# The first feed-forward bias enters as a 32-row product in PSUM instead of a VectorE step

## What is computed

```python
h = layernorm(x, ln1_g, ln1_b)                    # 256 channels
h = bitlinear(h, w1, b1)                          # 256 -> 1024
h = jax.nn.gelu(h, approximate=False)
h = layernorm(h, ln2_g, ln2_b)                    # 1024 channels
h = bitlinear(h, w2, b2)                          # 1024 -> 256

def bitlinear(x, w, b):     # x rounded to 127 levels per token, w to -1, 0, 1
    return einsum('btd,hd->bth', act_quant_fake(x), weight_quant_fake(w)) + b
```

## Time and profile before

| | before |
|---|---|
| timed runs | 394.05, 397.33, 396.52 |
| median | 396.52 |
| the profiled execution | 393.59, its span 391.8 |
| granted PE clock over the span | 0.995 |
| PE busy | 335.9 (86%) |
| DVE busy | 305.9 (78%) |
| ACT busy | 264.4 (67%) |
| POOL busy | 184.4 (47%) |

### The profile page before, as it was taken

One profiled execution on the slowest core, in us unless ns is written; L12 is line 12 of the kernel. 1 busy time (PEld: TensorE's weight loads), 2 busy tenths in 40 slices (PEclk: granted clock), 3 DMA queues, 4 the chain that ended last, 5 costly groups with the idle time before them and its releaser, 6 DMA issues.

```text
span 391.8 us, 9333 instructions
## 1 busy us (share of the span) xinstructions
PE 335.9 (86%) x3173; PEld 239.8 (61%) x3173; DVE 305.9 (78%) x1026; ACT 264.4 (67%) x567; POOL 184.4 (47%) x207
## 2 busy tenths in 40 slices
PE   7999789999999999967577877867977999999976
PEld 6777566776777677623444554545545666666654
DVE  3998846777898998788999899897346877877884
ACT  2656345466545545757689998988667888888843
POOL 2115301111211375248999899884104555456470
PEclk9999999999999999999899999999999999999999
DMA  7999999979464360000000000000001122212101
GB/s 242 304 271 263 275 239 235 233 151 258 127 127 89 92 99 3 1 2 0 1 3 0 0 2 1 3 0 2 1 2 32 38 43 55 49 37 54 43 14 55
DMA packets 44142, 33.70 MB, mean 86 GB/s; under 512 B 19904, under 2 KB 40256, under 8 KB 43968
## 3 DMA queue, kind: packets, MB, share of 16 engines
q1 hardware_dynamic: 44096, 33.11, 34.5%
HBM read 24.71 MB, written 8.39 MB: 84 GB/s over the span
## 4 chain that ended last, share of the span: by engine, by line
PE 53%; DVE 20%; issue 13%; ACT 8%; POOL 3%; DMA 1%; SPq 0%; DVEq 0%; POOLq 0%; ACTq 0%
PE PS L1340 5%; PE PS L1433 5%; PE PS L1422 4%; PE PS L1670 4%; DVE sm L784 4%; PE PS L1413 4%; PE PS L1412 4%; PE PS L1493 4%; PE PS L1662 4%; PE PS L1452 4%; DVE sm L756 3%; ACT pT L1115 2%; PE PS L1632 2%; PE PS L1655 2%; PE PS L1621 2%
## 5 line engine op out<-in xcount | busy, mean ns | idle before, releaser
L1115 ACT ACTIVATE pT<-PS 128x512 f32<-128x512 f32 x64 | 36.5, 596 | 48.2 <-PE PS L1413 47.9
L645 DVE TENSOR_REDUCE negm<-PS 128x4 bf16<-128x512 f32 x64 | 42.3, 684 | 13.0 <-PE PS L1422 12.8
L445 POOL TENSOR_TENSOR sm<-sm,mhalf 128x1 f32<-128x1 f32 x16 | 11.4, 711 | 80.6 <-DVE sm L677 80.6
L467 POOL TENSOR_TENSOR kst<-kst,rows 128x1024 f32<-128x1024 f32 x16 | 38.0, 2375 | 7.7 <-ACT kst L1159 7.7
L1237 ACT ACTIVATE lnT<-PS,Atok 128x128 f32<-128x128 f32 x128 | 36.4, 369 | 1.9 <-DVE lnb L901 0.8
L1413 PE MATMUL PS<-identb,negm 128*128 128x128 bf16 x256 | 34.9, 220 | 0.0
L1540 PE MATMUL PS<-identf,w2f 128*128 128x128 f32 x128 | 18.3, 288 | 18.2 <-ACT w2f L1182 18.2
L484 POOL TENSOR_TENSOR kst<-kst,rows 128x1024 f32<-128x1024 f32 x14 | 33.2, 2368 | 0.0
L1433 PE MATMUL PS<-pT,vx 128*32 128x128 f32 x512 | 27.0, 285 | 5.2 <-ACT pT L1115 5.2
L1540 PEld LDWEIGHTS PS<-identf,w2f 128*128 128x128 f32 x128 | 14.4, 146 | 22.9 <-ACT w2f L1182 21.5
L512 POOL TENSOR_TENSOR rr<-ms,mhalf 128x8 f32<-128x8 f32 x16 | 26.3, 1648 | 1.9 <-DVE ms L983 1.9
(11 more groups left out here) (228 smaller groups left out, 999.1 us busy)
## 6 DMA issues: line engine op xcount, KB each, us to landing
scr_q<-qpart SPq DMA_DIRECT2D x8, 384.0 KB, 3.4
scr_k<-kpart SPq DMA_DIRECT2D x8, 384.0 KB, 4.5
X<-in_x SPq DMA_DIRECT2D x8, 256.0 KB, 5.1
CTXT<-in_ctxT SPq DMA_DIRECT2D x8, 256.0 KB, 5.2
vx<-in_ctx SPq DMA_DIRECT2D x16, 128.0 KB, 3.1
out<-rest SPq DMA_DIRECT2D x16, 128.0 KB, 1.7
rows<-in_rows SPq DMA_DIRECT2D x1, 1544.0 KB, 10.0
qst<-scr_q SPq DMA_DIRECT2D x8, 192.0 KB, 4.8
```

What stands on the lines that cost most here:

```text
L467: gp.tensor_tensor(n2[q.slot], n2[q.slot], ln2g, ALU.mult).then_inc(b_g2, 1)
L645: v.tensor_reduce(negm[f.slot % 2][:, 4 * hg:4 * hg + 4], PS[:, 2 + hg % 2, :].rearrange("p (h k) -> p h k", h=4), AX_X, ALU.max, negate=T ...
L1115: s.activation(pT[:, hg, :], PS[:, hg % 2, :], ACT.Exp, scale=float(DH0) ** -0.5).then_inc(a_e, 1)
```

## The change

The bias b1 is split into three bfloat16 parts, and so is the reciprocal of each token's scale (unit times mean weight). Six of 32 rows hold the pairs of parts whose products count; the other rows are zero. A product of `ivT` (32 rows, the token's reciprocal) with `b1p` (32 rows, the bias) adds bias over scale to the up product in PSUM, and the gelu multiplies by the scale as it reads PSUM. `hidden` and its row of scaled bias go. Four batches share one 128-row transpose of the reciprocals, so batch a uses the rows 32(a mod 4) to 32(a mod 4)+31.

```diff
+            def bias_rest(i):
+                dve.wait_ge(b_bm, i + 1)
+                v.scalar_tensor_tensor(out=b1r, in0=b1p[:], scalar=b1m[:, 2 * i:2 * i + 1], in1=b1r,
+                                       op0=ALU.mult, op1=ALU.add).then_inc(b_b1, 1)
+            def inverse_parts(g):
...
+                ilink(v.tensor_scalar(uw[:, four], unit1[:, four], wmean[:, 0:1], None, ALU.mult))
+                ilink(v.reciprocal(iv[:], uw[:, four]))
+                for k in range(3):
+                    ilink(v.tensor_copy(ivp[:, :, k], iv[:]))
+                    if k < 2:
+                        ilink(v.tensor_tensor(iv[:], iv[:], ivp[:, :, k], ALU.subtract))
+                v.tensor_copy(ivp[:, :, 3:5], ivp[:, :, 0:2]).then_inc(b_ip, 1)
+                v.tensor_copy(ivp[:, :, 5], ivp[:, :, 0]).then_inc(b_ip, 1)
 # DVE, attention turn, before update(c)
-                if c and c.b == NB - 2:
-                    hidden(Turn(0, 0, 0))
+                if c and c.b in (NB - 4, NB - 3):
+                    bias_rest(c.b - (NB - 4))
+                if c and c.b == NB - 3:
+                    inverse_parts(0)
 # DVE, feed-forward turn
-                if b and b.b > 1:
-                    hidden(b)
...
+                if tau in (2, 5, 9):
+                    inverse_parts((2, 5, 9).index(tau) + 1)
 # ACT
+                if a.b % 4 == 0:
+                    s.activation(ivT[a.b // 4 % 2][:], PS[:, 4, 256:384], ACT.Copy).then_inc(b_iT, 1)
+            def bias_part(i):
+                act.wait_ge(s_rows2, 16)
+                act.wait_ge(c_z, 1)
+                if i:
+                    act.wait_ge(b_b1, i)
+                s.activation(b1p[:], b1r, ACT.Copy, scale=(1.0, 1.0, b1m[:, 1:2])[i]).then_inc(b_bm, 1)
...
+                if c and 11 <= c.b < 14:
+                    bias_part(c.b - 11)
                 if e:
                     level(e)
             def gelu(b):
-                act.wait_ge(b_hb, b.b + 1)
+                act.wait_ge(b_m1, b.b + 1)
-                s.activation(gl[b.slot], hb[b.slot], ACT.Gelu, scale=wmean[:, 0:1]).then_inc(b_gl, 1)
+                s.activation(gl[b.slot], PS[:, 2:4, :].rearrange("p a n -> p (a n)"), ACT.Gelu,
+                             scale=uw[:, b.b:b.b + 1]).then_inc(b_gl, 1)
...
                 if a:
                     columns(a)
+                if b:
+                    gelu(b)
                 if g:
...
-                if b:
-                    gelu(b)
-                if p and p.b > 0:
+                if p:
                     normed(p, tau)
 # PE, up(a)
-                done(pe, b_hb, a, 0)
+                done(pe, b_gl, a, 0)
+                quarter = slice(32 * (a.b % 4), 32 * (a.b % 4) + 32)
                 for n in range(2):
                     for kc in range(KC):
-                        last = t.matmul(PS[:, 2 + n, :], hT[:, kc, :], w1q[:, kc, n * 512:(n + 1) * 512],
-                                        start=(kc == 0), stop=(kc == KC - 1))
+                        t.matmul(PS[:, 2 + n, :], hT[:, kc, :], w1q[:, kc, n * 512:(n + 1) * 512], start=(kc == 0), stop=False)
+                    last = t.matmul(PS[:, 2 + n, :], ivT[a.b // 4 % 2][quarter, :], b1p[quarter, n * 512:(n + 1) * 512],
+                                    start=False, stop=True)
 # PE, attention turn of c = 15: up(1) and columns(2) now stand behind wo
-                    if c.b == NB - 1:
-                        up(Turn(1, 1, 0))
...
-                    if c.b == NB - 1:
-                        columns(Turn(2, 2, 0))
...
                     last.then_inc(a_o, 1)
+                    if c.b == NB - 1:
+                        up(Turn(1, 1, 0))
+                        columns(Turn(2, 2, 0))
```

More of the change, by code:

```diff
@@ L183, in chunks @@
             return w.rearrange("(c p) n -> p c n", p=128)
-        hb = 2 * [pT[:, 2 * i:2 * i + 2, :].rearrange("p a n -> p (a n)") for i in range(2)]
         gl = 2 * [qst[i].rearrange("p h t -> p (h t)").bitcast(F32) for i in range(2)]
@@ L199, in build @@
         hT = sb("hT", [128, KC, S], BF16)
+        b1p = sb("b1p", [128, F], BF16); b1m = sb("b1m", [128, 3]); ehot = sb("ehot", [128, 32])
+        uw = sb("uw", [128, NB]); iv = sb("iv", [128, 4]); ivp = sb("ivp", [128, 4, 32], BF16)
+        ivT = [sb(f"ivT{i}", [128, S], BF16) for i in range(2)]
         sm1 = [sb(f"sm1_{i}", [128, 16]) for i in range(2)]
@@ L213, in build @@
         b_t1 = sem("b_levels_transposed"); b_hT = sem("b_hT_ready")
-        b_m1 = sem("b_up_done"); b_hb = sem("b_hidden_ready"); b_gl = sem("b_gelu_ready")
+        b_ip = sem("b_inverse_parts_ready"); b_it = sem("b_inverse_turned"); b_iT = sem("b_inverse_rows_ready")
+        b_i = sem("b_inverse_chain"); b_bm = sem("b_bias_masks_ready"); b_b1 = sem("b_bias_chain")
+        b_m1 = sem("b_up_done"); b_gl = sem("b_gelu_ready")
         b_c2 = sem("b_stats2_chain"); b_c4 = sem("b_stats3_chain"); b_mv = sem("b_ones_placed")
@@ L431, in _ @@
                 step(gp.memset(vx2[i][:, :, DH1:64], 1.0))
+            step(gp.memset(ivp[:], 0.0))
+            step(gp.tensor_tensor(ehot[:], identf[:, 0:32], identf[:, 32:64], ALU.add))
+            step(gp.tensor_tensor(ehot[:], ehot[:], identf[:, 64:96], ALU.add))
+            step(gp.tensor_tensor(ehot[:], ehot[:], identf[:, 96:128], ALU.add))
+            step(gp.tensor_tensor(b1m[:, 0:1], ehot[:, 3:4], ehot[:, 4:5], ALU.add))
+            step(gp.tensor_tensor(b1m[:, 0:1], b1m[:, 0:1], ehot[:, 5:6], ALU.add))
+            step(gp.tensor_tensor(b1m[:, 1:2], ehot[:, 0:1], ehot[:, 1:2], ALU.add))
+            step(gp.tensor_tensor(b1m[:, 1:2], b1m[:, 1:2], ehot[:, 2:3], ALU.add))
+            step(gp.tensor_tensor(b1m[:, 1:2], b1m[:, 1:2], b1m[:, 0:1], ALU.add))
+            step(gp.tensor_scalar(b1m[:, 0:1], b1m[:, 0:1], -1.0, None, ALU.mult))
+            step(gp.tensor_scalar(b1m[:, 2:3], ehot[:, 5:6], -1.0, None, ALU.mult))
             gp.memset(junk[:, 0:2], 0.0).then_inc(c_z, 1)
             def scale_rows(i):
-                row, by = ((b1r, wscale[:, 0:1]), (ln2g, wmean[:, 1:2]), (ln2b, wmean[:, 1:2]))[i]
+                row, by = ((ln2g, wmean[:, 1:2]), (ln2b, wmean[:, 1:2]))[i]
                 pool.wait_ge(s_rows2, 16)
@@ L454, in turn_a @@
                     residual(d)
-                    if 9 <= d.b < 12:
+                    if 9 <= d.b < 11:
                         scale_rows(d.b - 9)
@@ L842, in _ @@
             spreads(first, None, 1)
-            hidden(Turn(1, 1, 0))
             update(last)
@@ L1186, in turn_b @@
                                  ACT.Copy).then_inc(b_QT, 1)
-                if p and p.b == 0:
-                    normed(p, tau)
-                if b:
-                    gelu(b)
-                if p and p.b > 0:
+                if p:
                     normed(p, tau)
@@ L1386, in columns @@
                 done(pe, b_hT, a, 0)
+                if a.b % 4 == 0:
+                    pe.wait_ge(b_ip, a.b // 2 + 2)
+                    t.matmul(PS[:, 4, 256:384], ivp[:].rearrange("p a k -> p (a k)"), identb[:], start=True, stop=True).then_inc(b_it, 1)
                 for i in range(KC):
```

24 lines of the change are left out of this document (14 added, 10 removed).

## The result

The changed kernel takes **422.75 us** (median of 4 runs, 421.99 to 424.26) against 396.53 of the kernel before (4 runs): ratio **1.068**, 95% interval 1.062 to 1.073. The profiled execution has a span of 421.0 us against 391.8. The forecast was 405.5 with a range to 409.5: right in sign, wrong by 17 us.

What follows compares the result with a forecast made beforehand. Engines waiting for each other in a turn, a loop of DVE's scale2, ACT's u2, QT and gelu, and DVE's statistics, bound the kernel; +3.3 entry, +7.9 nine turns, -1.0 exit made +10.2 on 395.4: 405.5 us, range 399.5 to 409.5.

Steps and rivals of the forecast that it cites:

- Part 1: Attention turns: DVE's added bias steps and first inverse_parts make the last attention turn go on 3.3 us late.
- Part 2: PE's two added 32-row products: 0.40 us each, including 0.09 each way for changing row count.
- q: PE time a batch for the two 32-row products: 0.79 us, bounds 0.43 and 1.11.
- Part 3: ACT's gelu reading PSUM: 1.09 us, 1.00 from start to start, bounds 0.91 and 1.05.
- Part 4: Full feed-forward turns: gelu ahead of u2 closes a loop over PE, 6.96 us against 6.07; nine turns +7.9.
- Part 5: First feed-forward turns: POOL's first multiply 5.9 late, then no gaps, removed step pays 0.9; +3.3 at u2 of batch 3.
- Part 6: Way out after u2 of batch 12: gelu no longer stands between u2 and normed, -1.0 us.
- The clock: Full turns: a granted clock well below 1.00 would lengthen PE's 3.04 + q of the loop; not priced into the sum.
- The rivals: Cheap products about 401.7 (0.20); tail waits about 409 (0.16); loop not binding 397 to 398 (0.09); faster 391 (0.05).
- The reason given for no gain: Full turns: removed L743, 1.28 us, lies where DVE would otherwise wait for u2 and gelu, so without it DVE waits longer.

Runs made afterwards that it cites:

- gelu_late: The changed kernel with ACT's gelu put back behind the columns of Q, ahead of the normed rows; 416.84 us, ratio 1.057.
- tt_parts: The changed kernel with the reciprocal's parts made in DVE's TENSOR_TENSOR form; 423.82 us, ratio 1.073.
- filled_waits: The changed kernel with 24 and 16 PE filler products ahead of the transposes of u2 of batches 2 and 6; 415.20 us, ratio 1.055.
- remedied kernel: The changed kernel with gelu put back, bias parts begun earlier, reciprocal parts moved into waits, and the 16 fillers behind batches 2 and 3 removed; 399.44 us, ratio 1.015.
- filled_entry: The remedied kernel with 10 and 6 PE filler products added ahead of the up products of batches 2 and 3; 396.15 us, ratio 1.004.

## Why the prediction was wrong

**Right.** Part 1: ACT's second `bias_part` waits for DVE and the exponentials start at 156.17 (forecast 156.25); the value products of the last attention turn start at 165.02 (165.0 or 165.1); `inverse_parts` of group 0 took 1.65 (1.6). Part 2: q 0.83 for 0.79. Part 3: gelu 1.11 for 1.09, and 1.00 from start to start as said. Part 4: the loop over PE exists, 7.06 for 6.96, and goes when gelu goes back (gelu_late). Part 5 up to POOL's first multiply: 178.35 for 178.2. Part 6: 0.8 came back for 1.0. The 0.9 us that Part 5 gives to the removed step at the entry was tested by no run.

**The step that failed is Part 5 behind that multiply, with the same omission in Part 4.** "From there it works without a gap" was not so, and groups 1 to 3 of `inverse_parts` have no term anywhere: Part 4 gives batches 8 and 12 only PE's 0.06 and ACT's 0.2, since DVE, "6.07 less the idle and the step that goes", was taken to have 2 us to spare in a turn. It has them, but not there: the chain stands between the statistics and scale2, ahead of u2. What the runs put in its place: these groups alone cost the kernel before 17.4 us, and 11.9 in the one-input forms that pass beside POOL; in those forms they bring the changed kernel from 1.068 to 1.046.

Here a page bears that I had not applied. The changed kernel's rows show 4-element CASTs and COPYs, and in tt_parts a TENSOR_TENSOR, ending with POOL's operation, and a RECIPROCAL and TENSOR_REDUCEs passing beside it. The Trainium skill (SBUF — State Buffer, Who interferes with whom) says that DVE and GpSimd share a pair of SBUF ports, that fast copies, casts and scalings need it, and so do operations with two SBUF inputs while GpSimd reads SBUF, and that whoever comes second stands for the whole instruction, while a TENSOR_REDUCE never does. Beside POOL's operations of 1024 columns the rows agree, form by form. Beside its 128x2 one of 0.70 us (L495, 203.83) they do not: a TENSOR_TENSOR and a CAST passed in 0.17 and 0.18.

**The clock**, which the prediction named and did not price, is the second missing term: 3.7 us behind the two long waits (filled_waits), 1.5 in the turn of 8.54, and 3.3 in the remedied kernel's entry (399.44 to 396.15). Up to u2 of batch 0, 11.0 late, the entry of the changed kernel is PE's path and not group 1's: scale2 of that batch ends at 189.19 and u2 starts at 192.78, with no idle time before it, behind `columns` and gelu. The clock makes the eight fillers behind `up` 3.59 us long, and `columns` of batch 3 waits for them: 184.22 against 174.22 in the kernel before, 10.0 late where the forecast path was 6.0 late. Group 2 comes on top: from u2 of batch 1 to that of batch 2 it is 10.75 instead of 6.35. I had followed DVE and POOL there, and not PE's fillers in the list of what stands in a row.

**The rivals.** None had this mechanism. q between the bounds was as forecast. The reason given for no gain holds: what goes, L743, is worth nothing in a full turn: with everything put right (filled_entry) the turns are 6.06 from u2 of batch 8 to that of batch 11, as before.

What is shown is the size of each edit alone; they do not add (1.057 and 1.055 give 1.056 together), and I have no full division of the 26 us.

## What to carry to other kernels

Price an added chain of tiny instructions at the place where it stands, not against its engine's mean spare time: ahead of a value that another engine waits for, 3.2 us cost 4.0 on the average of three places; moved into waits, with gelu back in its place and fillers ahead of `up`, the chains left the kernel within 0.4% of the one before. Ask of each added DVE instruction whether POOL runs something long then, and if so use forms that passed here, RECIPROCAL, TENSOR_REDUCE and one-column scalings. Behind a new wait of PE such as those of 6.81 and 7.41 us here, price what follows at half rate as well. Put filler products into such a wait, and not between a product and the next one that others wait for.
